# First stage and the start of the attention: constant rows by DMA, x loaded ahead of the weights, first keys and queries from ScalarE's queue, one general wait replaced by single ones

## What is computed

```python
def _ada_ln(x, cond, W, b):
    ss = cond @ W + b
    scale, shift = jnp.split(ss[:, None, :], 2, axis=-1)
    return _ln(x) * (1.0 + scale) + shift
h = _ada_ln(x, cond, Wln1, bln1)
q, k, v = heads(h @ Wq + bq), heads(h @ Wk + bk), heads(h @ Wv + bv)   # 16 heads of 32
attn = softmax(einsum('bhqd,bhkd->bhqk', q, k) / sqrt(32))
x = x + (attn @ v, heads joined) @ Wo + bo
h = _ada_ln(x, cond, Wln2, bln2)
x = x + gelu(h @ W1 + b1) @ W2 + b2
x = graph attention of x
```

## Time and profile before

| | us |
|---|---|
| median of 3 runs (3295.88 to 3303.61) | 3295.89 |
| profiled execution | 3315.78 |
| its span, first to last instruction | 3314.2 |
| busy in the span: PE, DVE, POOL, ACT | 3211.7, 2079.5, 1436.7, 1391.1 |
| mean granted TensorE clock of the span (1 is full) | 0.978 |
| first stage, to the last value product | about 375.6 |
| attention (value matmuls L659) | from 389.4 |

### The profile page before, as it was taken

The page is one execution under the profiler, slowest core; times in us unless marked ns, Lnnn a source line. Parts: engine busy times, 40 slices in busy tenths (PEclk is TensorE's granted clock), DMA queues, the critical chain, the costliest instruction groups (busy, mean ns, idle before and its releaser), DMA issues.

```text
span 3314.2 us, 44368 instructions
## 1 busy us (share of the span) xinstructions
PE 3211.7 (97%) x16890; PEld 2200.4 (66%) x16890; DVE 2079.5 (63%) x3537; ACT 1391.1 (42%) x2703; POOL 1436.7 (43%) x656
## 2 busy tenths in 40 slices
PE   8798999999999999999999998899999999999999
PEld 7686655555555555555555545688888888778888
DVE  4647778778788787787878775543333332226766
ACT  2121366666666566665666663221111111012222
POOL 0200478778787786776867763210000000002222
PEclk9899999999999999999999999999999999889999
DMA  5474488888988788797887877520111112201221
GB/s 195 143 221 141 142 196 199 183 187 191 205 180 199 186 186 199 174 205 183 186 200 171 193 175 214 197 92 15 39 38 39 39 39 79 77 22 64 73 78 58
DMA packets 185883, 464.12 MB, mean 140 GB/s; under 512 B 27164, under 2 KB 69276, under 8 KB 154183
## 3 DMA queue, kind: packets, MB, share of 16 engines
q0 software_dynamic: 31968, 232.80, 31.5%
q1 hardware_dynamic: 153703, 228.49, 23.3%
HBM read 151.90 MB, written 75.76 MB: 69 GB/s over the span
## 4 chain that ended last, share of the span: by engine, by line
PE 86%; DMA 7%; DVE 3%; issue 2%; ACT 1%; POOL 1%; SPq 1%; DVEq 0%; POOLq 0%; ACTq 0%
PE ps L372 13%; PE ps L647 13%; PE ps L659 12%; PE ps L1178 11%; PE ps L1165 11%; DMA accd<-pt 5%; PE ps L446 4%; PE ps L1712 4%; PE ps L665 3%; PE ps L1725 3%; PE ps L450 2%; PE ps L1746 1%; PE ps L1541 1%; PE ps L1029 1%; DMA ao<-ao_d 1%
## 5 line engine op out<-in xcount | busy, mean ns | idle before, releaser
L385 DVE TENSOR_REDUCE nmp<-ps 128x1 f32<-128x512 f32 x1966 | 1202.2, 680 | 169.5 <-PE ps L372 168.1
L716 ACT ACTIVATE pt<-ps 128x512 f32<-128x512 f32 x2048 | 1033.4, 627 | 556.6 <-PE ps L647 556.5
L822 POOL TENSOR_TENSOR pacc<-pacc,pt 128x2048 f32<-128x2048 f32 x186 | 882.1, 4742 | 37.7 <-ACT pt L716 32.7
L647 PE MATMUL ps<-qs,ks 128*128 128x512 f32 x2048 | 817.3, 403 | 4.4 <-issue 4.0
L372 PE MATMUL ps<-ks,qs 96*128 96x512 f32 x1966 | 811.5, 413 | 3.3 <-POOL ones L798 3.3
L372 PEld LDWEIGHTS ps<-ks,qs 96*128 96x128 f32 x1966 | 377.8, 192 | 271.0 <-DVE nmp L385 162.7
L659 PE MATMUL ps<-pt,vq 128*32 128x512 f32 x4096 | 492.5, 598 | 0.0
L647 PEld LDWEIGHTS ps<-qs,ks 128*128 128x128 f32 x2048 | 393.8, 193 | 99.6 <-ACT pt L716 16.6
L1165 PE MATMUL ps<-hpb,w 128*128 128x512 f32 x1536 | 382.8, 399 | 3.4 <-DMA x_d<-x 3.4
L1178 PE MATMUL ps<-w,gp 128*128 128x512 f32 x1536 | 380.5, 396 | 2.3 <-DVE gp L1314 2.3
L1178 PEld LDWEIGHTS ps<-w,gp 128*128 128x128 f32 x1536 | 289.4, 188 | 71.7 <-DVE gp L1314 2.8
(11 more groups left out here) (175 smaller groups left out, 3180.9 us busy)
## 6 DMA issues: line engine op xcount, KB each, us to landing
accd<-pt POOLq DMA_DIRECT2D x222, 1024.0 KB, 9.1
qk_d<-st SPq DMA_DIRECT2D x128, 256.0 KB, 2.7
ks<-qk_d SPq DMA_DIRECT2D x24, 1024.0 KB, 16.0
qs<-qk_d SPq DMA_DIRECT2D x96, 256.0 KB, 6.8
xina<-in_x SPq DMA_DIRECT2D x8, 1024.0 KB, 6.4
v_d<-vst SPq DMA_DIRECT2D x32, 256.0 KB, 2.3
vq<-v_d SPq DMA_DIRECT2D x8, 1024.0 KB, 14.0
recb<-r_d SPq DMA_DIRECT2D x32, 256.0 KB
```

What stands on the lines that cost most here:

```text
L385: dve.tensor_reduce(nmp[:, n // 4, n % 4:n % 4 + 1], ps[:, ring.bank["max", u], :], AX.X, ALU.max, negate=True).then_inc(s_mr, 1)
L647: pe.matmul(ps[:, score_bank(n), :], ksb[w % 2][:, hh, 128 * kt:128 * kt + 128], qsb[:, v % 3, hh, :], start=True, stop=True).then_inc(s_s ...
L716: act.activation(pt[:, g % 8, hh, :], ps[:, score_bank(n), :], ACT.Exp, scale=SCALE).then_inc(s_exp, 1)
L822: pool.tensor_tensor(pacc[:, :, :], first, pt[:, g % 8, :, :], ALU.add).then_inc(s_add, 1)
```

## The change

It leaves the arithmetic as it is and changes orders, queues and waits.

- The pads of ks and qs are copied by two DMAs, which POOL issues at the place of the memsets, from a small tile `pad` that POOL fills at the very start; the pad of the second ks is copied from the first by DMA at the start of the attention. s_pad counts 16 for each.
- At the start SP issues condT, the biases and x ahead of the weights. PE does scale-shift 0 and 1, transposes 0 and 1, scale-shift 2 and 3, transposes 2 and 3. VectorE scales ahead of its scale-shift work. The splits of Wq alternate with the turns on ScalarE and VectorE. The statistics of chunk 1 stand between the splits of Wk and Wv, its scaling after those of Wv.
- The first keys are issued by ScalarE in chunk 4 after products 3, 5 and 7, the queries of sets 0, 1 and 2 by ScalarE in chunk 5 after products 1, 3 and 5.
- The values of the first heads are loaded by SP in the last chunk ahead of product 4. For that hpa1 is placed ahead of hpa0 and xina, so that the values lie over buffers that are free by then.
- PE, ScalarE and VectorE begin the attention without qkv_over; PE waits for single banks, ScalarE for what its pt buffers overlay; ones is written ahead of POOL's qkv_over, and PE waits for it at the first sums.

```diff
--- before.py
+++ after.py
@@ -220,12 +220,14 @@
         bln = take("bln", [128, 2, 8])
         bvB = take("bvB", [128, D])
         bqk = take("bqk", [128, 2, NK])
-        fa = Front(nc, fsems, 0, take("xina", [128, NK, D]), take("hfa", [128, 2, CH]),
-                   [take(f"hpa{i}", [128, 2, NK, CH], F32R) for i in range(2)], shared)
+        hpa1 = take("hpa1", [128, 2, NK, CH], F32R)
+        hpa0 = take("hpa0", [128, 2, NK, CH], F32R)
+        fa = Front(nc, fsems, 0, take("xina", [128, NK, D]), take("hfa", [128, 2, CH]), [hpa0, hpa1], shared)
         wtmp = take("wtmpa", [128, 4, D])
         wqkv = [take("w" + n, [128, 2, NK, D], F32R) for n in "qkv"]
         st = take("st", [128, 8, CH], F32R)
         vst = take("vst", [128, 4, D])
+        pad = take("pad", [128, CH])
 
         s_wt = [sem(f"s_wt{j}") for j in range(4)]
         s_bias = sem("s_bias")
...
@@ -345,13 +342,15 @@
 
         def sp_row(v):
             sp.wait_ge(s_nh, 2 * v + 2)
-            sp.wait_ge(s_pad, 3)
+            sp.wait_ge(s_pad, 32)
             for r in range(2):
                 sp.dma_start(qsb[96 + r:97 + r, v % 3, :, :].bitcast(F32), nmr[:, r, :].bitcast(F32)).then_inc(s_md, 16)
 
         def pe_bank_free(what):
 
             if ring.before[what] is None:
+                if ring.bank[what] < 6:
+                    pe.wait_ge(s_vev, 4 * NC8 - 5 + ring.bank[what])
                 return
...
@@ -414,12 +413,13 @@
             step = 0
             pe_scale_shift(0, 0, 7)
             pe_scale_shift(0, 1, 6)
-            pe_scale_shift(0, 2, 5)
             pe.wait_ge(s_ident, 16)
             fa.pe_turn(0, 0, 0)
+            fa.pe_turn(0, 1, 1)
+            pe_scale_shift(0, 2, 5)
             pe_scale_shift(0, 3, 4)
-            for k in range(1, NK):
-                fa.pe_turn(0, k, k % 2)
+            fa.pe_turn(0, 2, 0)
+            fa.pe_turn(0, 3, 1)
             for ci in range(NC8):
                 hp = fa.hp[ci % 2]
                 if ci == 1:
@@ -462,10 +462,9 @@
         def act_qkv():
             for i in range(3):
                 for k in range(NK):
+                    if i == 0:
+                        fa.act_turn(0, k, k % 2)
                     act_split(4 * i + k, wqkv[i][:, 0, k, :], wtmp[:, k, :], s_wt[k], 16 * (i + 1))
-                if i == 0:
-                    for k in range(NK):
-                        fa.act_turn(0, k, k % 2)
             act.wait_ge(s_bias, 48)
             for ci in range(NC8):
                 for j in range(8):
@@ -479,23 +478,32 @@
                         act.wait_ge(s_ql, u - 3)
                     act.activation(st[:, r0, :], ps[:, 2 + (12 * ci + j) % 4, :], ACT.Identity,
                                    bias=bqk[:, j // 4, j % 4:j % 4 + 1]).then_inc(s_qh, 1)
+                    if ci == NCH and j in (3, 5, 7):
+                        if j == 3:
+                            for i in range(8):
+                                act.wait_ge(s_qst[i], 128)
+                            act.wait_ge(s_pad, 32)
+                        load_k(act, 0, j // 2 - 1)
+                    if ci == NCH + 1 and j in (1, 3, 5):
+                        load_q(act, j // 2)
 
         def dve_qkv():
             step = 0
             fa.dve_stats(0, range(NK))
+            fa.dve_scale(0, range(NK))
             dve_scale_shift(0, 0, 7)
             dve_scale_shift(0, 1, 6)
-            fa.dve_scale(0, range(NK))
-            dve_scale_shift(0, 2, 5)
-            for k in range(NK):
-                dve_split(k, wqkv[0][:, 1, k, :], wtmp[:, k, :], wqkv[0][:, 0, k, :])
-            for k in range(NK):
-                if k == 1:
-                    dve_scale_shift(0, 3, 4)
-                fa.dve_turn(0, k)
-            for i in (1, 2):
+            for i in range(3):
                 for k in range(NK):
+                    if i == 0:
+                        fa.dve_turn(0, k)
+                        if k == 0:
+                            dve_scale_shift(0, 2, 5)
+                            dve_scale_shift(0, 3, 4)
                     dve_split(4 * i + k, wqkv[i][:, 1, k, :], wtmp[:, k, :], wqkv[i][:, 0, k, :])
+                if i == 1:
+                    fa.dve_stats(1, range(NK))
+            fa.dve_scale(1, range(NK))
             dve.wait_ge(s_bias, 48)
             for ci in range(NC8):
...
@@ -503,11 +511,11 @@
                         dve_scale_shift(1, k, 7 - k % 2)
                 for j in range(12):
                     if j < 8 and ci + 1 < NC8:
-                        if j < 2:
+                        if j < 2 and ci:
                             fa.dve_stats(ci + 1, (2 * j, 2 * j + 1))
-                        elif j < 4:
+                        elif 2 <= j < 4 and ci:
                             fa.dve_scale(ci + 1, (2 * j - 4, 2 * j - 3))
-                        else:
+                        elif j >= 4:
                             if j == 4 and ci:
                                 dve.wait_ge(s_vm, 4 * ci)
                             fa.dve_turn(ci + 1, j - 4)
@@ -533,26 +541,24 @@
                             dve.wait_ge(s_vst[t], 16 * ci)
                         dve.tensor_tensor(vst[:, t, :], ps[:, bank, :], bvB[:, :], ALU.add).then_inc(s_vev, 1)
 
-        def pool_pad(t, bias_rows):
-
-            pool.memset(t[96:128].bitcast(F32), 0.0).then_inc(s_pad, 1)
-            if bias_rows:
-                pool.wait_ge(s_pad, bias_rows - 1)
-                pool.memset(t[96:98].bitcast(F32), 1.0).then_inc(s_pad, 1)
-                pool.wait_ge(s_pad, bias_rows)
-
         def pool_qkv():
+
             pool.memset(mhalf[:, :], -0.5).then_inc(s_mh, 1)
+            pool.wait_ge(s_mh, 1)
+            pool.memset(pad[96:128, :], 0.0).then_inc(s_mh, 1)
+            pool.wait_ge(s_mh, 2)
+            pool.memset(pad[96:98, :], 1.0).then_inc(s_mh, 1)
+            pool.wait_ge(s_mh, 3)
             fa.pool_rstd(0)
             for ci in range(NC8 - 1):
                 fa.pool_rstd(ci + 1)
                 if ci == 1:
                     pool.wait_ge(s_ssv, 16)
                     pool.wait_ge(s_ssp, 16)
-                    pool.wait_ge(fa.s_rstd, 3)
-                    pool_pad(ksb[0], 2)
-                    pool_pad(qsb, 0)
-                    pool.wait_ge(s_pad, 3)
+                    pool.dma_start(ksb[0][96:128, :, :].bitcast(F32).rearrange("p h (c n) -> p (h c) n", n=CH),
+                                   pad[96:128, :].unsqueeze(1).to_broadcast([32, 16, CH])).then_inc(s_pad, 16)
+                    pool.dma_start(qsb[96:128, :, :, :].bitcast(F32).rearrange("p s h n -> p (s h) n"),
+                                   pad[96:128, :].unsqueeze(1).to_broadcast([32, 12, CH])).then_inc(s_pad, 16)
 
         def sp_load_x(ci):
             if ci:
@@ -560,12 +566,20 @@
             sp.dma_start(fa.xin[:, :, :],
                          x_d[CH * ci:CH * ci + CH, :].rearrange("(t p) d -> p t d", p=128)).then_inc(fa.s_x, 16)
 
+        def sp_load_v(w):
+            b, f = w // 4, 128 * (w % 4)
+            sp.dma_start(vq[:, w % 2, :, :],
+                         v_d[S * b:S * b + S, f:f + 128].rearrange("(t p) e -> p t e", p=128)).then_inc(s_vq[w % 2], 16)
+
         def sp_qkv():
             step = 0
+            sp.dma_start(condT[:, :, :], a["condT"].rearrange("(k p) b -> p k b", p=128)).then_inc(s_sml[0], 16)
+            sp.dma_start(bln[:, 0, :], a["bln1c"]).then_inc(s_sml[0], 16)
+            sp_load_x(0)
             sp_load_ss(0, (0, 2))
             sp.dma_start(ident[:, :], a["c_ident"]).then_inc(s_ident, 16)
-            sp_load_x(0)
             sp_load_ss(0, (1, 3))
+            sp.dma_start(bln[:, 1, :], a["bln2c"]).then_inc(s_sml[1], 16)
             for i, name in enumerate(("Wq", "Wk", "Wv")):
                 if i == 1:
                     sp.dma_start(bvB[:, :], row("bv")).then_inc(s_bias, 16)
@@ -581,16 +595,12 @@
             for ci in range(NC8):
                 b, c = divmod(ci, NCH)
                 for j in range(12):
-                    if ci == NCH and j == 1:
-                        for r in range(8):
-                            sp.wait_ge(s_qst[r], 128)
-                        sp.wait_ge(s_pad, 3)
-                    if ci == NCH and j in (1, 3, 5):
-                        sp_load_k(0, j // 2)
-                    if ci == NCH and j in (6, 7):
-                        sp_load_q(j - 6)
-                    if ci == NCH + 2 and j == 0:
-                        sp_load_q(2)
+                    if ci == NC8 - 1 and j == 4:
+                        for t in range(4):
+                            sp.wait_ge(s_vst[t], 16 * NCH)
+                        sp.wait_ge(s_vm, 4 * (NC8 - 1))
+                        sp.wait_ge(fa.s_turn, NK * NC8)
+                        sp_load_v(0)
                     if j == 8 and ci + 2 < NC8:
                         sp_load_x(ci + 2)
...
@@ -669,6 +679,7 @@
 
             bank = ring.bank["sums", v]
             pe_bank_free(("sums", v))
+            pe.wait_ge(s_on, 1)
```

(20 more changed lines are left out.)

28 lines of the change are left out of this document (9 added, 19 removed).

## The result

The changed kernel takes 3285.43 us (median of 13 runs, 3267.35 to 3298.21) against 3301.55 for the kernel before, run in turn with it on the same chip. The ratio is 0.9954, with a 95% interval from 0.9932 to 0.9976. So it is faster, by 16 us and not by the 28 of the forecast. Its profiled execution has a span of 3279.1 us at a mean granted clock of 0.987 (before 3314.2 and 0.978).

What follows compares the result with a forecast made beforehand. PE, busy 97% of the span, was taken as the bound, with gains only where it stands still. The terms -17.9 - 7.5 - 5.1 + 2.5 gave -28.0 us, from the median 3295.89 to 3267.9; range 3257 to 3287.

Steps and rivals of the forecast that it cites:

- Hole A: Chunk 1, PE waiting 16.94 us for its first transpose while memsets on POOL hold up VectorE's scaling: -17.9 us.
- Rival 2: Chunk 1: the pads' DMA issue blocks VectorE as the memsets did, all of Hole A stays, 3286 us; chance 0.07.
- Hole B: Chunk 5, PE waiting 7.41 us for late x; keys and queries moved to ScalarE's queue, and later: -7.5 us.
- rival 1: Chunk 6's x stays late, waiting for bytes and not the queue; 7.5 us not gained, 3275 us; chance 0.15.
- Hole C: Start of the attention: waits for single banks replace one wait for everything, first value product earlier: -5.1 us.
- rival 3: The attention begins no earlier, values or row of maxima landing late on SP's queue; 5.1 us not gained, 3273; chance 0.08.
- Nothing there: Second ks's pad, copied by DMA beside the attention instead of memsets: PE waits for neither, so no gain or loss.
- The start: First chunk, x ahead of the weights: first product 4.8 us later, part given back by the K products, +2.5 us.
- they reach the end one for one: All four terms lie ahead of stages where PE is never free, so all 28.0 us reach the end.
- Rival 4: Without pauses the granted clock falls where PE is busy; a fall of 0.013 costs 42 us, 3310; chance 0.04.

Runs made afterwards that it cites:

- pads_only: The kernel before with only the memsets of the pads in chunk 1 replaced by POOL's two DMAs: 3295.01 us, ratio 0.9969.
- keys_on_sp: The changed kernel with the first keys and queries issued on SP's queue again, at the new places: 3284.26 us, ratio 0.9954.
- one_wait: The changed kernel with the general wait before the attention back, and the first values loaded after it: 3288.9 us, ratio 0.9967.
- ks1_dma_only: The kernel before with only the second ks's pad changed, one DMA in place of two memsets: 3309.66 us, ratio 1.0025.
- old_start: The changed kernel with the first 45 us as in the kernel before, x behind the first weights: 3284.43 us, ratio 0.9957.
- both_pads: The kernel before with its chunk 1 memsets kept and POOL's two pad DMAs added behind them: 3312.53 us, ratio 1.0022.
- lag_before: ks1_dma_only with one wait changed, so that POOL issues its first accumulating DMA in unit 0 some 6 us later: 3314.8 us, ratio 1.003.
- ks1_memset: The changed kernel with the second ks's pad written by two memsets on POOL again, instead of a DMA: 3288.42 us, ratio 0.9976.
- act_all: The changed kernel without any pad DMA or pad memset, ScalarE writing all pads: 3291.45 us, ratio 0.9976.

## Why the prediction was wrong

It gave -28.0 us, 3268 and a range from 3257 to 3287; measured are -16 and 3285.43. That lies inside the outer range only because it was stretched for rivals 1 to 3, none of which came about as told; the forecast's own range, 3260 to 3277, is missed. What holds and what fails is seen term by term.

**Hole A, -17.9:** right, and too small. pads_only gives 21.0. The issues beside the scaling were bounded by 0 and 4 us; they show as 0.94 and 0.64 us on POOL and hold up nothing. The 3 us more lie about in these pieces: the 1 us taken for those issues, 0.75 in hole B (6.66 us long in pads_only), 1.7 in a half-rate stretch ahead of hole A (6.8 us long instead of 10.2 in the record of the granted clock). Rival 2 is out; by the Trainium skill's rule in SBUF — State Buffer, section "Who interferes with whom", the 14.47 us were the exclusion of VectorE by a whole memset, and the 1.08 us without them agree.

**Hole B, -7.5:** 5.3 by its rows, and rival 1 is half right. x goes out 1.9 us behind the last key load and is not there in the assumed 7 to 9 us but in 14.2; the queue had nothing to do with it (13.5 us in keys_on_sp). What helped is the earlier issue against PE's need. This agrees with the rule quoted from the Trainium skill, DMA: Bandwidth & Descriptors, section "Issuing engines are not separate DMA queues". The failed step was taking x's median for its load beside keys that another queue carries.

**Hole C, -5.1:** 5.2 from the end of the stage to the first value product (8.6 for 13.8), 6.9 against one_wait. Right, and rival 3 is out. The line "Nothing there" on the pads of ks1 was a costly one: replacing the memsets costs 8.0 us in ks1_dma_only. They stood inside hole C, where nothing waited for them.

**The start, +2.5:** the steps came as told (x used at 7.25 for 7.4, first product at 30.37 for 31.4, keys at 44.68 for 45.3), and up to the end of chunk 4 the new start costs 3.0 us against old_start, near the 2.5 of the term, though 1.7 of them are half rate, which it did not count. At the first value product 0.4 are left, because the earlier kernel loses more in hole B. What the term had wrong is that it was added to hole B as if the two were apart. That the four terms add up so well is in part luck: hole A gained 3 us more, hole B 2 less, and the start lost 2 less.

**The sum and its last step.** The four terms came to -28.8 where the forecast had -28.0. The step that failed is the one behind them: "they reach the end one for one", since PE is never free later. PE is busy in 1590.9 of the attention's 1620.7 us; but the other 30 (20.6 for accumulating DMAs, 4.6 for POOL's sums, 4.0 with no releaser in the profile) and the 19 of the output stage (15.5 for VectorE, 3.4 for a store) are waits, and they aren't constants, nor is the time at half rate. All 16 kernels that differ from before gave something back, 0.5 to 21 us, whether the edit removed work, moved it or added some (both_pads), and whether the attention began earlier, at the same time, or 81 us later. What the runs show in its place: of the 28.8 us, 12.4 are given back, 7.3 in waits and work and 5.1 in time at half rate. Changing ks1's pad alone costs 8, and the pads' way through POOL's queue some 5; these are separate measurements and don't simply add, since pads_only, which keeps ks1's memsets, gives back 10. Why a memset at 378 us shortens an output stage at 2010 us is **not settled**: it isn't POOL's lag (lag_before), nor the small store (ks1_memset has a short one and gives back as much), nor the DMA itself (act_all). That the arrangement of before happens to suit its own later waits is a reading that fits the part in waits; it was argued, not shown. Why more time at half rate follows an earlier attention is open as well.

**Rival 4, the clock:** the other way in the whole, its own way behind the first stage. Weighted by each execution's granted clock, the mean span falls from 3237.7 to 3231.6 us, so 6 of the 16 us are work and waits and 10 are less time at half rate (63.5 us lost to it before, 53.2 after). The first stage alone loses 15.4 less (its clock went from 0.94 to 0.98, first rows of the two tables); the stages behind it lose 5.1 more, which is a mean clock of 0.984 for 0.986. The rival was priced on the whole span and left out that a stage could gain clock while the rest loses some.

## What to carry to other kernels

When holes ahead of a nearly full stage are closed, take the gain at the next marker and measure the rest by itself: here 28.8 us stood at the marker and 16 at the end. A full engine still has a few per cent of waits that aren't constants (here mostly for DMAs of another engine), and edits far ahead move them; the time at half rate moves too. So don't count on one for one (here 5 to 15 us went in most kernels, over 2900 us of such stages). Work that stands in a hole is free; if the hole is closed, ask anew where it belongs. And a delay ahead of a wait that lasts doesn't add to it: most of what the start lost here was hidden by hole B.

## What the runs showed of the hardware

The 8 KB store of the last unit but one took 4.7 to 5.6 us or 14.5 to 16.3 us, and nothing between, over all 20 profiles. It is a matter of this one store: the median of the 32 stores of its line is 6.4 to 7.0 us in every profile, and where it is short none of them takes over 8.8 us. DMA packets by queue around it, from 1983 to 1990 us in the kernel before and from 1954 to 1972 us in the changed one:

```profile
q0 software_dynamic: 172, 1.28, 67.8%
q1 hardware_dynamic: 690, 1.00, 38.5%
```
```profile
q0 software_dynamic: 379, 2.71, 65.0%
q1 hardware_dynamic: 701, 1.02, 15.4%
```

In both some 700 packets of SP's queue (1.0 MB) pass. From the store's issue to the next alone, 5.58 and 16.34 us, it is 0.9 MB of SP's queue both times, beside 0.86 MB of POOL's accumulating DMAs in the first and 2.36 in the second; over all profiles it is 0.66 to 0.86 MB beside the short store and 2.36 to 2.52 beside the long one. So the long one lasts until well over a megabyte more of them has passed; that it waits for these bytes was not shown. Its issue stands at the same distance from POOL's in all 20 (0.10 to 0.12 us ahead of an accumulating DMA), so what decides isn't visible there.

The other surprise is that idle time of PE at the start gave the clock nothing: 112 us without a matmul left the time lost at half rate no smaller (59 us against 53), and hole A was worth 21.0 us where it had lasted 16.94, 1.9 us of it because PE had gone on at half rate behind it.
